# One wait ahead of the loads of the long cross attention

## The chip, the cores and the metric

The kernel runs on one core of a Trainium2 chip. The metric is the device time of one execution in microseconds (us), lower is better. The engines are TensorE (PE, its weight loads shown as PEld), VectorE (DVE), ScalarE (ACT), GpSimd (POOL) and SyncE (SP). SP issues every plain DMA of this kernel, POOL issues the indirect ones (scatters and gathers). All DMAs of both share 16 DMA engines.

## The reference, cut to what matters

Two decoder layers on x (32 batches, 56 tokens, width 128), with a context of 1500 tokens per batch:

```python
x = x + attn0(layernorm(x))                       # stage 0
x = x + cross_attn0(layernorm(x), ctx, ctx, ...)  # stage 1
x = x + experts_top2(layernorm(x), ...)           # stage 2, capacity limited
x = x + running_softmax_attn(layernorm(x), ...)   # stage 3: num/den of cumulative sums
x = x + cross_attn1_rope(layernorm(x), ctx, ...)  # stage 4: the long cross attention, 1500 keys
x = x + experts_sigmoid_top2(layernorm(x), ...)   # stage 5
```

Stage 2 sends each token to two of eight experts and adds up the two results, weighted:

```python
out = ye[idx1, pos1] * (w1 * keep1)[:, None] + ye[idx2, pos2] * (w2 * keep2)[:, None]
```

Stage 3 needs that sum, row by row, before its own layer norm. Stage 4 needs keys and values, which are products of the context alone (`ctx @ Wk.T` with a rotary embedding, `ctx @ Wv.T`).

## The kernel before, in words

The 32 batches are padded to 64 rows and stacked two to a tile, so x is 16 tiles of 128 rows (`XR`). The kernel is written without a planner: each engine has its own program, written out by hand, and `program` walks through the six stages in order on every engine. Where stage k starts, an engine first waits for the end marks of an earlier stage, then runs the *next* stage's preparation (`load` on SP), then stage k's own part. So the loads of stage 4 are issued by SP at the start of stage 3, right behind the last result writes of stage 2 (L1133). The order within SP's queue is the order of the code, and nothing behind a waiting instruction is issued.

**The load of stage 4** (`load` in `l1_xattn`) issues 14 DMAs (L2008), all counted by one semaphore, `c1_in`: five weights of 64 KB, a small mask, the cosine and sine tables (750 KB each), two small tables, and then in pairs `c_ones` (562.5 KB) and `c_zero` (256 KB). Each of these four fills writes 16 partitions alone, with one long row per partition (36,000 and 16,384 bytes). Nine DMAs of the context follow (L2004, `fetch`): three chunks of 250 KB for each of the batches 0, 1 and 2. Every consumer of these loads waits for all 14 (`c1_in(len(loads))`), and the keys and values of batch 0 also for its three context chunks (`ctx_of`).

**The late gathers.** The expert results of stage 2 lie in DRAM (`results`). Two indirect DMAs per tile of rows (L1524, `gather`) fetch them into `XT`, and DVE adds them to `XR` in `combine` (L1383). The tiles 0 to 7 are gathered within stage 2, beside its second half. The tiles 8 to 15 (chunk 1) are gathered in stage 3, by POOL: `LATE_GATHER` says at which step t of stage 3: 0: tiles 8, 9, 10; 1: tiles 11, 12; 2: tiles 13, 14; 3: tile 15. The semaphores `gathered[j]` count tile j and tile j + 8, so `gathered[j](4)` is reached when tile j + 8 has landed as well.

**Stage 3** (`l1_attn`) runs over t = 0 to 19 and keeps one pipeline across the engines: at step t PE projects the values of tile t (L1599), ACT copies them out (L1624), DVE multiplies (L1728) and PE forms running sums (L1672), DVE (L1737, L1741) and POOL (L1795) make the output of tile t - 1, PE turns it (L1683) and multiplies by the output weight (L1691), DVE adds it to `XR` (L1745). DVE also combines the late tiles: 8 and 9 at t = 1, 10 and 11 at t = 2, and so on (`LATE_NORM`). Their norm goes through DVE (L118 to L122), POOL (L127), DVE (L143), PE (L151) and ACT (L156) a step or two later. In POOL's queue an item waits for all items ahead of it: at step t = 2, for instance, the multiply L1795, the four gather DMAs of tiles 13 and 14, and then the norm's power L127 of tiles 8 and 9.

**Early work of stage 4 within stage 3.** From t = 5 on, the engines also run steps of stage 4 (`early`): the keys of batch 0, first chunk, at t = 5 (PE, L2096), values at t = 6 (L2105), the blend with cosine and sine on DVE (L2225) and POOL (L2362, L2368), and so on to t = 19. PE meets the first of them between the transposes of step 5. It is there that PE waits for `c1_in` and for the context of batch 0. SP's own part of stage 3 (`early_sp`) stands behind the loads in its queue. Its first item writes key parts at t = 11 (L2044).

Of the kernel before, what the change touches and what calls it, by code (L numbers as in the profile page):

```python
# [59 lines left out]
def decoder(nc, a, out):  # L60
    with ExitStack() as ctx:
# [5 lines left out]
        def signal(name, total, step=1, over=None):  # L67

            name = over or name
            if name not in sems:  # L70
                sems[name] = [ctx.enter_context(nc.semaphore(name)), 0]
            s = Signal(sems[name][0], sems[name][1], step)
            sems[name][1] += total * step
            return s
# [951 lines left out]
        def l0_ffn():  # L1026
# [65 lines left out]
            gathered = [signal("gathered%d" % j, 4, 16) for j in range(8)]  # L1092
            combine_mul = signal("combine", 2 * NT, over="based")
            combined = lambda t: combine_mul(2 * t + 2)
# [437 lines left out]
            def pool(e, w):  # L1532
                for n in range(16):
                    scatter(e, w, 1, n)
                for j in range(10):
                    if j >= 2:
                        ln_power(e, w, 3, j - 2)
                    if j < 8:
# [1 line left out]

            return Stage(load=load, prep_pool=prep_pool, early_sp=early_sp, early_pe=early_pe, early_dve=early_dve, early_act=early_act,
                         early_pool=early_pool, sp=sp, pe=pe, dve=dve, act=act, pool=pool, gather=gather, combine=combine,
                         combined=combined,
                         end=lambda: [y_cp(NI), down_mm(NI), gated(4 * NI), kept(11), w_cp(NI)] + chunk_out(1))


# [269 lines left out]
        def l1_xattn():  # L1816
# [185 lines left out]
            def fetch(e, b, ch):  # L2002
                sl = slice(500 * ch, 500 * ch + 500)
                e.dma_start(C[:, b % 3, sl], a["ctxT"][b][:, sl]).then_inc(ctx_in[b % 3].sem, 16)  # L2004

            def load(e, w):
                for dst, src in loads:
                    e.dma_start(dst, src).then_inc(c1_in.sem, 16)  # L2008
                for b in range(3):
                    for ch in range(3):  # L2010
                        fetch(e, b, ch)
# [381 lines left out]
            def early_pool(e, w, t, kinds):  # L2393
                for step in early(t):
                    if step[0] in kinds:
                        pool_step(e, w, step)

            return Stage(load=load, chore_pool=chore_pool, between=between, early_sp=early_sp, early_pe=early_pe, early_dve=early_dve,
                         early_act=early_act, early_pool=early_pool, sp=sp, pe=pe, dve=dve, act=act, pool=pool,
                         end=lambda: ln_done(5) + [joined(NT)])  # L2400
# [87 lines left out]
        stages = []  # L2488
        for k, f in enumerate((l0_attn, l0_xattn, l0_ffn, l1_attn, l1_xattn, l1_ffn)):
            place.update(used=642 if k == 5 else 0, low=k % 2 == 0 or k == 5)  # L2490
            stages.append(f())
# [136 lines left out]
```

## Time and profile before

| | us |
|---|---|
| median of 3 runs | 1534.07 |
| lowest, highest | 1530.72, 1545.25 |
| the profiled execution | 1527.03 |
| its span, first to last instruction | 1525.2 |
| mean granted TensorE clock | 0.951 of full |
| PE, DVE, POOL, ACT busy | 89%, 72%, 54%, 54% |

The profiled execution is 7.0 us below the median of the timed runs. Times in the rows are us from the start of the span. `SPq` rows are DMAs that SP issues; their duration is the issue, not the transfer. A number in brackets is the idle time ahead of an instruction, with what ended it. `PEclk` 1.00 is 2.4 GHz and 0.50 is 1.2 GHz. A DMA row gives the median time from issue to landing.

### The profile page before, as it was taken

To read this page: it belongs to the slowest core of one execution; us is meant where nothing else is said; L and a number is where in the kernel's file an instruction comes from. 1 tells how busy PE (TensorE), PEld (TensorE's weight loads), DVE (VectorE), ACT (ScalarE), POOL (GpSimd) and SP (SyncE) were. 2 spreads that over 40 slices of the span, in tenths; PEclk is the share of its full clock that TensorE was granted. 3 is DMA by queue.
4 is the path that set the end of the run, shared out by engine and by line. 5 is a ranking of instruction groups with operands and counts; after the bars stand their busy time and mean duration, and the time that the engine had idled before them with its cause. 6 is when DMAs were issued, how large, how long until landed. Compare 5 with 4: busy or idle time off the path is not lost.

```text
span 1525.2 us, 41823 instructions
## 1 busy us (share of the span) xinstructions
PE 1358.7 (89%) x17179; PEld 927.0 (61%) x17179; DVE 1093.6 (72%) x1832; ACT 821.8 (54%) x1804; POOL 825.7 (54%) x736
## 2 busy tenths in 40 slices
PE   6788999998967996759999999999999999789998
PEld 4567788788935663335666566656665666555554
DVE  6885767656747887747888888888888888435554
ACT  3442334355622331436777777777777777733332
POOL 6665322424654675747778777877787774000000
PEclk9868999999987998779999999999999999989999
DMA  4004400032271034364555554555464554305230
GB/s 128 2 1 128 159 2 2 19 85 86 65 153 39 1 71 78 75 118 124 125 124 133 118 129 123 133 118 132 121 133 118 128 123 93 96 3 111 61 61 13
DMA packets 76511, 134.71 MB, mean 88 GB/s; under 512 B 18017, under 2 KB 56034, under 8 KB 73058
## 3 DMA queue, kind: packets, MB, share of 16 engines
q1 hardware_dynamic: 74274, 127.84, 35.0%
q0 software_dynamic: 2048, 4.20, 1.0%
q8 instruction: 137, 2.24, 0.7%
q14 instruction: 52, 0.43, 0.1%
HBM read 100.54 MB, written 34.73 MB: 89 GB/s over the span
## 4 chain that ended last, share of the span: by engine, by line
PE 35%; POOL 12%; ACT 8%; issue 3%; DVE 3%; DMA 1%; SPq 0%; ACTq 0%; POOLq 0%; DVEq 0%
PE ps L2158 8%; POOL ARENA L2362 8%; PE ps L916 7%; PE ps L2142 5%; POOL ARENA L2368 4%; PE ps L928 4%; PE ps L2105 3%; ACT ARENA L2312 3%; PE ps L2096 2%; ACT ARENA L2290 2%; PE ps L2119 2%; ACT ARENA L2303 2%; ACT ARENA L2296 1%; PE ps L2167 1%; DVE ARENA L2232 1%
## 5 line engine op out<-in xcount | busy, mean ns | idle before, releaser
L2232 DVE TENSOR_REDUCE ARENA<-ps 112x2 f32<-112x1000 f32 x384 | 456.4, 1197 | 122.6 <-PE ps L2119 119.8
L2312 ACT ACTIVATE ARENA<-ps 125x448 f32<-125x448 f32 x768 | 378.4, 549 | 129.0 <-PE ps L2142 128.4
L2362 POOL TENSOR_TENSOR ARENA<-ARENA 64x500 f32<-64x500 f32 x192 | 264.6, 1378 | 106.4 <-ACT ARENA L2290 88.2
L2142 PEld LDWEIGHTS ps<-ARENA 64*125 64x125 bf16 x3072 | 122.9, 134 | 134.6 <-ACT ARENA L2312 70.7
L2142 PE MATMUL ps<-ARENA 64*125 64x112 bf16 x3072 | 169.6, 229 | 19.9 <-ACT ARENA L2312 18.7
L2158 PE MATMUL ps<-ARENA 125*17 125x112 f32 x6144 | 185.5, 261 | 0.0
L2119 PE MATMUL ps<-ARENA 64*112 64x500 bf16 x768 | 153.4, 388 | 9.8 <-DVE ARENA L2232 9.4
L127 POOL TENSOR_TENSOR rs<-rs,mhalf 128x1 f32<-128x1 f32 x96 | 71.7, 750 | 161.1 <-DVE rs L122 160.8
L2158 PEld LDWEIGHTS ps<-ARENA 125*17 125x17 f32 x6144 | 136.7, 97 | 32.1 <-issue 21.9
L2368 POOL TENSOR_TENSOR ARENA<-ARENA 128x500 f32<-128x500 f32 x96 | 147.1, 1533 | 8.1 <-DVE ARENA L2225 0.7
L2373 POOL TENSOR_TENSOR ARENA<-ARENA 128x500 bf16<-128x500 f32 x96 | 111.0, 1157 | 37.7 <-ACT ARENA L2296 37.7
L2096 PE MATMUL ps<-ARENA 128*128 128x500 f32 x192 | 108.2, 647 | 14.6 <-DMA ARENA<-in_ctxT 13.7
L916 PE MATMUL ps<-XT,ARENA 128*128 128x448 f32 x288 | 115.6, 546 | 0.0
L2105 PE MATMUL ps<-ARENA 128*125 128x128 f32 x768 | 109.8, 287 | 1.2 <-ACT ARENA L1624 1.2
L2105 PEld LDWEIGHTS ps<-ARENA 128*125 128x125 f32 x768 | 92.7, 189 | 26.2 <-issue 21.7
L2225 DVE TENSOR_TENSOR ARENA<-ARENA 128x500 f32<-128x500 f32 x96 | 89.8, 935 | 3.5 <-ACT ARENA L2290 3.5
L916 PEld LDWEIGHTS ps<-XT,ARENA 128*128 128x128 f32 x288 | 55.1, 193 | 53.0 <-issue 52.6
L2290 ACT COPY ARENA<-ps 128x500 f32<-128x500 f32 x96 | 55.6, 580 | 48.1 <-PE ps L2096 42.3
L2296 ACT CAST ARENA<-ARENA 128x500 bf16<-128x500 f32 x96 | 58.5, 610 | 35.8 <-POOL ARENA L2368 30.1
L156 ACT COPY XT<-ps 128x128 f32<-128x128 f32 x96 | 25.6, 271 | 91.1 <-PE ps L151 91.1
L1009 DVE TENSOR_TENSOR ARENA<-ps,ARENA 128x448 f32<-128x448 f32 x72 | 44.8, 623 | 41.2 <-PE ps L916 39.8
L789 POOL TENSOR_TENSOR ARENA<-ARENA 128x896 f32<-128x896 f32 x16 | 27.0, 1687 | 81.2 <-DVE ARENA L718 81.2
(273 smaller groups left out, 2384.7 us busy)
## 6 DMA issues: line engine op xcount, KB each, us to landing
ARENA<-key_parts SPq DMA_DIRECT2D x192, 187.5 KB, 3.9
ARENA<-in_ctxT SPq DMA_DIRECT2D x96, 250.0 KB, 3.7
key_parts<-ARENA SPq DMA_DIRECT2D x64, 375.0 KB, 2.6
ARENA<-token_weights SPq DMA_DIRECT2D x16, 512.0 KB, 5.3
slots<-in_c_blank SPq DMA_DIRECT2D x2, 1472.0 KB, 12.5
results<-ARENA SPq DMA_DIRECT2D x42, 64.0 KB, 1.6
ARENA<-in_L_ffn_W SPq DMA_DIRECT2D x1, 2048.0 KB, 8.7
ARENA<-in_L_ffn_W SPq DMA_DIRECT2D x4, 512.0 KB, 10.1
```

The costliest lines, as they stand in the source:

```text
L916: e.matmul(ps[:, bk, 0:448], wt(x, c), rhs, start=True, stop=True).then_inc(up_mm.sem, 1)
L2096: e.matmul(ps[:, b1, 0:500], wk, C[:, b % 3, 500 * ch:500 * ch + 500], start=True, stop=True) \
L2105: m = e.matmul(ps[0:KT, b1, 128 * k:128 * k + 128], C[:, b % 3, KT * kt:KT * kt + KT], wv, start=True, stop=True)
L2119: m = e.matmul(ps[0:112, b1 + h, 0:500], Q0[r, b % 3, g].rearrange("p j s -> p (j s)"), KS[b % 4][r, g, 500 * ch:500 * ch + 500], start=Tr ...
L2142: m = e.matmul(ps[0:KT, b1[h], 112 * g:112 * g + 112], KS[b % 4][r, g, KT * kt:KT * kt + KT], Q1[r, b % 2, 112 * g:112 * g + 112], start=T ...
L2158: m = e.matmul(ps[32 * c:32 * c + 17, 3, 112 * u:112 * u + 112], V[b % 3][0:KT, kt, x, :], Pb[0:KT, n % NP_, 112 * x:112 * x + 112], start ...
L2225: e.tensor_tensor(T1[:, n % 3, :], T0[:, n % 2, :], cos[:, 500 * ch:500 * ch + 500], ALU.mult) \
L2232: e.tensor_reduce(mxp[0:112, b % 2, 2 * g:2 * g + 2, ch], ps[0:112, b1:b1 + 2, 0:500], AX, ALU.max) \
L2312: e.activation(Pb[0:KT, n % NP_, 448 * h:448 * h + 448], ps[0:KT, b1[h], 0:448], ACT.Exp, bias=0.0, scale=1.0).then_inc(exped.sem, 1)
L2362: e.tensor_tensor(T2[r:r + 64, :], T0[64 - r:128 - r, n % 2, :], sin[64 - r:128 - r, sl], ALU.mult) \
L2368: e.tensor_tensor(T1[:, n % 3, :], T1[:, n % 3, :], T2, ALU.add).then_inc(k_sum.sem, 1)
L2373: e.tensor_tensor(Kl[:, sl], T1[:, (3 * b + ch) % 3, :], Kh[:, sl], ALU.subtract).then_inc(k_lo.sem, 1)
```

## The change: eight waits ahead of the loads

Stage 2 publishes a list of eight marks, one for each `gathered` semaphore, at their final count. SP waits for all eight before it issues the first of the 14 loads of stage 4. No load, buffer or size changes, and their order stays.

```diff
@@ l0_ffn
             return Stage(load=load, prep_pool=prep_pool, early_sp=early_sp, ...
-                         combined=combined,
+                         combined=combined, late=lambda: [g(4) for g in gathered],
@@ l1_xattn
             def load(e, w):
+                for mark in stages[2].parts["late"]():
+                    w.wait_ge(*mark)
                 for dst, src in loads:
                     e.dma_start(dst, src).then_inc(c1_in.sem, 16)
                 for b in range(3):
```

## Rows read from the trace of the kernel before

**Rows 1.** The page, busy time of each engine (share of the span), instructions.

```profile
PE 1358.7 (89%) x17179; PEld 927.0 (61%) x17179; DVE 1093.6 (72%) x1832; ACT 821.8 (54%) x1804; POOL 825.7 (54%) x736
```

**Rows 2.** Stretches: start:end, length, busy time of each engine, clock, DMA share, GB/s.

```profile
440.00:455.00 15.00, 5.52 (x9) 1.64 (x7) 5.08 (x10) 1.74 (x3) 11.24 (x11) 0.66 0.89 121
...
470.00:486.00 16.00, 10.10 (x37) 7.37 (x37) 11.23 (x31) 3.24 (x7) 6.82 (x9) 0.68 0.03 8
486.00:503.00 17.00, 16.64 (x95) 11.67 (x95) 13.73 (x26) 6.59 (x14) 8.34 (x8) 1.00 0.00 1
```

**Rows 3.** Chain that ended last: start, duration, engine and line.

```profile
582.73 1.80 PE ps L1691 x16
```

**Rows 4.** Timeline of SP's issues: start, duration, line.

```profile
427.58 0.33 SPq L2008 DMA_DIRECT2D ARENA<-in_L_xattn_WqT  x1
...
434.08 0.44 SPq L2008 DMA_DIRECT2D ARENA<-in_c_zero  x1
434.57 11.98 SPq L2004 DMA_DIRECT2D ARENA<-in_ctxT  x9
```

**Rows 5.** DMA issues about 434.2, 435.6, 432.2 and 470.2: us to landing last.

```profile
ARENA<-in_c_zero SPq DMA_DIRECT2D x1, 256.0 KB, 20.7
...
ARENA<-in_ctxT SPq DMA_DIRECT2D x1, 250.0 KB, 22.1
...
XT<-results,IDX POOLq DMA_INDIRECT x1, 14.2
...
XT<-results,IDX POOLq DMA_INDIRECT x1, 2.5
```

**Rows 6.** Timeline of DVE, the late combine and what stands around it.

```profile
437.68 1.22 DVE L1741 TENSOR_TENSOR ARENA<-ARENA 128x1024 f32<-128x1024 f32 x1 [0.73 <-POOL ARENA L1795]
...
446.39 0.74 DVE L1383 SCALAR_TENSOR_TENSOR XR<-XT,GW,XR 128x128 f32<-128x128 f32 x2 [6.10 <-DMA XT<-results,IDX]
...
458.95 1.36 DVE L143 TENSOR_SCALAR xn<-XR,mv,rs 128x128 f32<-128x128 f32 x2 [7.56 <-POOL rs L127]
```

**Rows 7.** Timeline of POOL, from the gather of tile 10 to that of tile 15.

```profile
437.73 2.03 POOL L1524 DMA_INDIRECT XT<-results,IDX  x1
...
451.53 1.90 POOL L1795 TENSOR_TENSOR ARENA<-ARENA 128x1024 f32<-128x1024 f32 x1 [2.17 <-DVE ARENA L1741]
...
458.32 1.10 POOL L127 TENSOR_TENSOR rs<-rs,mhalf 128x1 f32<-128x1 f32 x2
...
466.73 1.90 POOL L1795 TENSOR_TENSOR ARENA<-ARENA 128x1024 f32<-128x1024 f32 x1 [6.58 <-DVE ARENA L1741]
...
470.10 0.96 POOL L1524 DMA_INDIRECT XT<-results,IDX  x1 [0.30 <-issue]
```

**Rows 8.** Timeline of PE about its restart and about the first keys.

```profile
460.38 0.45 PE L151 MATMUL ps<-ident,xn 128*128 128x128 f32 x1 [6.36 <-DVE xn L143]
...
461.45 1.91 PE L1683 MATMUL ps<-ident,ARENA 128*128 128x128 f32 x8
463.16 2.78 PE L1691 MATMUL ps<-ARENA 128*128 128x128 f32 x16
...
486.11 1.01 PE L2096 MATMUL ps<-ARENA 128*128 128x500 f32 x2
...
487.07 1.03 PE L1683 MATMUL ps<-ident,ARENA 128*128 128x128 f32 x8
487.95 2.05 PE L1691 MATMUL ps<-ARENA 128*128 128x128 f32 x16
```

**Rows 9.** Finer stretches, the columns of rows 2.

```profile
457.50:460.00 2.50, 0.00 (x0) 0.00 (x0) 1.05 (x2) 0.00 (x0) 2.49 (x4) 0.61 1.05 367
460.00:462.50 2.50, 1.76 (x7) 1.50 (x8) 2.29 (x10) 0.53 (x2) 0.15 (x1) 0.50 0.50 181
462.50:465.00 2.50, 2.50 (x15) 2.50 (x14) 2.43 (x5) 1.17 (x2) 0.00 (x0) 0.52 0.00 0
465.00:467.50 2.50, 2.50 (x14) 1.54 (x13) 2.36 (x6) 0.00 (x0) 0.77 (x1) 1.00 0.00 0
```

## The prediction

> **What bounds the kernel now.** I read the page first. PE is busy 89% of the span [rows 1], but an average over six stages doesn't price a change at the border of two, so I went to the stretch that it touches: stretches of time from the end of stage 2 on, then each engine's timeline there, then the landings of the DMAs. Three things are to be seen. Between 440 and 486 us PE is far from full (5.5 of 15 us, then 10.1 of 16), while from 486 to 503 it is busy 16.6 of 17 us [rows 2]. The boundary is the first key product, at 486.11 us [rows 8]: ahead of it PE waits for others, behind it PE sets the pace. Second, the chain that ended last, followed back, is still in stage 3's own products (L1691) at 582.7 [rows 3], and stage 3's steps are a pipeline two buffers deep, so a delay of PE at 486 goes through to the end. Third, SP issues the stage 4 loads from 427.58 on [rows 4], far ahead of their first use.
>
> **What these loads cost now.** The second gather of tile 9 is issued at about 432.2 and takes 14.2 us to land, against 2.5 us for the last one of tile 15, issued when nothing else moves [rows 5]. DVE pays: its combine of tile 9 starts at 446.39 after 6.10 us of waiting for that landing [rows 6]. That is the only wait for a late gather that I find; the others land before DVE comes to them.
>
> **What the change gives back.** Without the loads beside it, that gather lands near 435, and DVE goes on 6.1 us sooner. But only part of it reaches the rest: the next thing in line is POOL's multiply L1795 at 451.53, which waited only 2.17 us for DVE and is behind POOL's own gathers otherwise [rows 7]. From there the chain is one of POOL's queue: gathers of tiles 13 and 14, then the power of tile 8's norm (458.32), then DVE's L143 at 458.95 (idle 7.56 us for POOL), then DVE's add, the multiply at 466.73, and the gathers of tile 15 [rows 6, 7]. So all of it moves by 2.17 us, not 6.1. A second gain is possible: the gather issue at 437.73 took 2.03 us where the last takes 0.96 [rows 7], which would make it 3.2 us if the busy DMA rings were the reason. It ran, however, exactly beside DVE's L1741, which starts at 437.68 and lasts 1.22 us [rows 6], and that stays. So I take 2.0 us as the gain at the moment at which tile 15 is gathered: the 2.17, and a little off. The bounds are 3.2 and 0, the latter if two such collisions of 1.1 us come in where DVE used to wait beside the gathers of tiles 11 and 12. The Trainium skill ("SBUF — State Buffer", SBUF: two separate sides) says that GpSimd and a DVE instruction with two SBUF inputs take turns on a shared port, the second one blocked until the first ends. By that rule the 1.1 us stay, and the sum would be nearer to the bound of 0; if it doesn't hold here, 3.2.
>
> **What the change costs.** The eight waits end with the last: `gathered[7]`, tile 15. Its second DMA is issued at 470.10 and lands 2.5 us on, at 472.6 [rows 5, 7]. With the gain it is 470.6. SP has nothing else queued there until the key parts of t = 11, so the waits cost nothing themselves; the semaphore hop I cost at 0.1, so the first load is issued at 470.7 instead of 427.58.
>
> How long from the first issue to usable data? Before, `c_zero`, the last of the 14, is issued at 434.08 and lands 20.7 us on, at 454.8. The third context chunk is issued two places behind 434.57, near 435.5, and lands 22.1 us on, at 457.6 [rows 4, 5]. Measured from the first issue that is 27.2 us for `c1_in` and 30.0 us for the context of batch 0, which PE needs too. Now the late gathers are out of the way. Ten DMAs of 64 KB (tiles 8 to 12) had landed by 457.6, 0.66 MB. At 367 GB/s, the rate at which contexts stream at 457.5 to 460 [rows 9], they are 1.8 us; at the mean 121 GB/s of 440 to 455 [rows 2] they would be 5.4 us. The low mean comes, I read, from the four fills, whose 16 long rows give each DMA engine one row of each fill, one behind the other, and these stay. So 28.2 us, with 24.6 and 30.0 as bounds.
>
> The key product then starts at 470.7 + 28.2 = 498.9 instead of 486.11: 12.8 us late. PE, which comes to it about 2 us earlier than before, stands idle from about 484 to 499. That is a new stall of some 15 us where 6.1 us of another engine's waiting was removed. DVE, POOL and ACT run out of work within a step, since step 6 needs step 5's products.
>
> **The clock after the stall** comes on top. When PE restarts at 460.38 after 6.4 us idle, the granted clock is 0.50 and then 0.52, and 1.00 from 465 on [rows 8, 9]. In that time eight transposes take 1.91 us and sixteen products 2.78, against 1.03 and 2.05 at full clock [rows 8]: 1.6 us for the two groups. As all the 4.6 us from restart to full clock would be dense now, at most 2.3 us are lost. I take 2.0.
>
> **The sum.** 12.8 + 2.0 = 14.8 us. The profiled execution of 1527.0 becomes 1541.8. It is 7.0 us under the median of the runs shown, 1534.1, so the median comes to 1548.9. Bounds of the case: 472.7 - 3.2 + 24.6 = 494.1 gives 8.0, with 1.6 for the clock 9.6 us; 472.7 + 30.0 = 502.7 gives 16.6, with 2.3 it is 18.9 us. So 1543.7 to 1553.0 as median.
>
> **The rivals.**
>
> *The loads land in time, and the kernel is not slower.* PE reaches the key product at 484.1, and SP starts at 470.7: the loads need 13.4 us or less. The loads and the first context are 4.37 MB, which at the 367 GB/s of [rows 9] is 11.9 us, and no stall is left; the gain of 2.0 us stands: 1525.0 in the profile, 1532.1 as median. The Trainium skill ("DMA: Bandwidth & Descriptors", Anatomy of one DMA) gives a fixed 2.0 us plus bytes at 436 GB/s, which makes 12.0 us and speaks for this rival. Against it stands the same list of DMAs in this trace: 30.0 us, when the gathers beside it moved only 0.66 MB. The rule would have to hold for 36,000-byte rows into 16 partitions. It decides at 13.4 us. Chance 0.07.
>
> *The stall is longer and the clock stays down.* The gathers of tile 15 come no sooner than before (collisions take all), the loads take the full 30.0 us, and PE, which alternates between short bursts and waits after the restart, is granted 0.50 for a whole step instead of 4.6 us. A stretch for it exists: between 470 and 486 PE was busy 10.1 of 16 us, and the clock averaged 0.68 [rows 2]. Price: 472.7 + 30.0 - 486.1 = 16.6 us, and a step of 8 us at half clock 4 us, 20.6 us: 1547.6 in the profile, 1554.7 as median. Against it: behind the stall PE is fed densely, as at 486 to 503. Chance 0.2.
>
> *Part is made up later.* Once PE restarts, DVE, POOL and ACT have caught up, and stage 3's last steps, where PE isn't full, swallow some of it. For it speaks that the gain of 6.1 us of DVE's is lost in just that manner. Against: a step ahead is all that two buffers allow. Price: half of the 12.8 us gone, +8.4 us, 1535.4 in the profile and 1542.5 as median. Chance 0.13.
>
> That the change does nothing is hardly possible: tile 15 is gathered after 468 in any case, SP would have to pass a semaphore that isn't there yet.
>
> **How the numbers follow.** The forecast of 1549 us has 0.6. One per cent is 15.3 us, about what a measurement of this kernel tells from no change, and 14.8 lies right under it; with the bounds of the terms and the spread of the runs (1530.7 to 1545.3) I give 0.45 of this case to over 1%. Slower by over 1%: 0.6 x 0.45 + 0.2 = 0.47. Within 1%: 0.33 + 0.13 + most of the first rival, 0.05: 0.51. Faster: 0.02. The range goes from 1539, under the case of partial recovery (1542.5) by what low runs may take off, to 1559, above the long stall.
>
> **What would show it.** In the trace of the changed kernel: SP's first L2008 near 470.7 instead of 427.58; the gather of tile 9 landing within 3 us and no idle time before L1383; POOL's multiply near 449.5 instead of 451.53, and the gather of tile 15 near 468; the idle time before PE's first L2096 near 15 us, put down to the context or the tables, with L2096 near 499; a clock of 0.50 for about 4.6 us behind it; and from there every instruction 14 to 15 us later than before, to the end. If the loads take a time far from 28 us, the term of the fills is wrong, and the result with it. If L2096 starts near 499 and the end moves by less than 12, the coupling of stage 3 is looser than I hold it to be.

## The result: 0.8% slower, 12 us at the median

| | before | changed |
|---|---|---|
| median of 20 runs, us | 1533.76 | 1545.97 |
| lowest, highest, us | 1523.82, 1545.25 | 1542.69, 1555.13 |
| profiled execution, us | 1527.03 | 1545.08 |
| its span, us | 1525.2 | 1543.3 |

The ratio is 1.0081, with a 95% interval of 1.0059 to 1.0104: 9 to 16 us slower. The forecast was 1548.9 us at the median, 14.8 us over the kernel before. The two profiled executions differ by 18.1 us, more than the medians do. How much of that is the change is taken apart below. One execution of the kernel before in a later group of runs took 1734.58 us at a mean granted clock of 0.734, where the others have about 0.95; it is in no median and no ratio here.

The profile after, from its page: the busy time of PE is 1360.4 us where [rows 1] had 1358.7, so the change adds no work, only waiting.

```profile
PE 1360.4 (88%) x17179; PEld 924.7 (60%) x17179; DVE 1096.3 (71%) x1832; ACT 821.7 (53%) x1804; POOL 825.0 (53%) x736
```

The stretches of the changed kernel that answer to [rows 2], and one more:

```profile
440.00:455.00 15.00, 6.25 (x16) 2.36 (x13) 7.63 (x12) 2.09 (x3) 13.16 (x12) 0.70 0.11 31
...
470.00:486.00 16.00, 9.52 (x37) 6.80 (x37) 12.26 (x34) 3.52 (x8) 6.20 (x9) 0.79 0.82 178
486.00:503.00 17.00, 3.76 (x12) 2.69 (x13) 3.18 (x3) 1.33 (x3) 2.92 (x3) 0.53 0.88 185
503.00:518.00 15.00, 14.64 (x83) 10.70 (x83) 8.86 (x19) 4.77 (x9) 5.59 (x5) 0.97 0.00 1
```

Between 486 and 503 us PE was busy 16.64 of 17 us; now it is 3.76, while the DMAs move 185 GB/s. SP's queue and the landings show why. The timeline of SP in the changed kernel, and the landings of the DMAs issued near 478.7 (`c_zero`) and 480.1 (third context chunk):

```profile
471.97 0.33 SPq L2010 DMA_DIRECT2D ARENA<-in_L_xattn_WqT  x1
...
479.08 8.06 SPq L2004 DMA_DIRECT2D ARENA<-in_ctxT  x9
```

```profile
ARENA<-in_c_zero SPq DMA_DIRECT2D x1, 256.0 KB, 18.6
...
ARENA<-in_ctxT SPq DMA_DIRECT2D x1, 250.0 KB, 19.1
```

The first load is issued at 471.97, not 427.58 [rows 4]. The third context chunk lands near 499.2, and PE's timeline has its first key product right there:

```profile
499.24 2.01 PE L2098 MATMUL ps<-ARENA 128*128 128x500 f32 x2 [14.17 <-issue]
501.04 0.42 PE L151 MATMUL ps<-ident,xn 128*128 128x128 f32 x1
501.25 1.92 PE L1683 MATMUL ps<-ident,ARENA 128*128 128x128 f32 x8
502.96 2.47 PE L1691 MATMUL ps<-ARENA 128*128 128x128 f32 x16
505.26 1.88 PE L1599 MATMUL ps<-ARENA,XT 128*128 128x512 f32 x4
```

Against [rows 8] the product starts at 499.24 instead of 486.11, after 14.17 us of idle time. The profile puts these down to "issue", not to a DMA; that the context lands at the same moment is what tells. The product, the transposes (L1683) and the output products (L1691) take 2.01, 1.92 and 2.47 us, where they took 1.01, 1.03 and 2.05 at full clock.

What the wait gives back is seen on DVE and POOL. First the timeline of DVE, with the combine of tiles 8 and 9 (L1383) without idle time, then that of POOL:

```profile
440.93 0.73 DVE L1383 SCALAR_TENSOR_TENSOR XR<-XT,GW,XR 128x128 f32<-128x128 f32 x2
...
442.31 3.17 DVE L1728 TENSOR_TENSOR ARENA<-ARENA 128x1024 f32<-128x1024 f32 x1
...
458.29 1.36 DVE L143 TENSOR_SCALAR xn<-XR,mv,rs 128x128 f32<-128x128 f32 x2 [10.39 <-POOL rs L127]
```

```profile
429.07 0.99 POOL L1524 DMA_INDIRECT XT<-results,IDX  x1 [5.61 <-DMA results<-ARENA]
...
442.48 1.91 POOL L1795 TENSOR_TENSOR ARENA<-ARENA 128x1024 f32<-128x1024 f32 x1
444.55 1.80 POOL L1524 DMA_INDIRECT XT<-results,IDX  x1 [0.16 <-issue]
...
450.83 1.92 POOL L1795 TENSOR_TENSOR ARENA<-ARENA 128x1024 f32<-128x1024 f32 x1
...
469.46 0.96 POOL L1524 DMA_INDIRECT XT<-results,IDX  x1 [0.30 <-issue]
```

The first late gather is at 429.07, where it was at 428.36: the changed kernel comes 0.71 us later to this border, by nothing that the change touches. With that taken off, POOL's multiply at 450.83 is 1.41 us earlier than in [rows 7], and so is the rest up to the last gather of tile 15 (469.46 for 470.10, 1.35 us). In [rows 6] DVE waited 6.10 us for the gather and 7.56 us for POOL ahead of L143, 13.66 us together; now it is 10.39 us for POOL alone. At PE's key product the gain is a little larger than at the gathers: PE is ready for it at about 484.9 instead of 486.1, which is 1.9 us earlier with the border taken off.

### The profile page after: what moved, and what is told of

Its sections match the earlier page's. It is cut to its first block, busy times and chain, and to the rows that moved or that the text cites. A ratio compares the mean times of both kernels' runs of the same rounds, so it can differ in the third digit from the quotient of the medians.

```text
span 1543.3 us, 41827 instructions
## 1 busy us (share of the span) xinstructions
PE 1360.4 (88%) x17179; PEld 924.7 (60%) x17179; DVE 1096.3 (71%) x1832; ACT 821.7 (53%) x1804; POOL 825.0 (53%) x736
## 4 chain that ended last, share of the span: by engine, by line
PE 36%; POOL 11%; ACT 8%; issue 3%; DVE 2%; DMA 1%; SPq 0%; ACTq 0%; POOLq 0%; DVEq 0%
PE ps L2160 8%; POOL ARENA L2364 7%; PE ps L916 7%; PE ps L2144 5%; POOL ARENA L2370 4%; PE ps L928 4%; ACT ARENA L2314 3%; PE ps L2107 3%; PE ps L2098 2%; ACT ARENA L2292 2%; PE ps L2121 2%; ACT ARENA L2305 1%; ACT ARENA L2298 1%; PE ps L2169 1%; DVE ARENA L2234 1%
## 5 line engine op out<-in xcount | busy, mean ns | idle before, releaser
L2370 POOL TENSOR_TENSOR ARENA<-ARENA 128x500 f32<-128x500 f32 x96 | 147.3, 1534 | 8.1 <-DVE ARENA L2227 0.7
L2098 PE MATMUL ps<-ARENA 128*128 128x500 f32 x192 | 110.7, 661 | 27.2 <-issue 14.2
L151 PE MATMUL ps<-ident,xn 128*128 128x128 f32 x80 | 27.3, 349 | 55.6 <-DVE xn L143 48.4
```

The lines of the kernel that those rows point to most:

```text
L2098: e.matmul(ps[:, b1, 0:500], wk, C[:, b % 3, 500 * ch:500 * ch + 500], start=True, stop=True) \
L2370: e.tensor_tensor(T1[:, n % 3, :], T1[:, n % 3, :], T2, ALU.add).then_inc(k_sum.sem, 1)
```

## The experiments

All are compared with the kernel before, run beside them on the same chip. As times of whole executions scatter, each profile is also read over one stretch that holds the change and ends when the clock is full again: from the first late gather (POOL, first L1524 of chunk 1) to the first values of batch 0 (PE, `values` at t = 6). Before, that is 428.36 to 494.07, 65.71 us.

| kernel | first late gather | first values | stretch, us | against before | ratio of times, 95% interval |
|---|---|---|---|---|---|
| before | 428.36 | 494.07 | 65.71 | | |
| changed | 429.07 | 509.49 | 80.42 | +14.7 | 1.0081 (1.0059 to 1.0104) |
| changed, again | 431.79 | 511.98 | 80.19 | +14.5 | 1.0123 (1.0077 to 1.0168) |
| wait for tiles 8 to 14 | 437.98 | 507.37 | 69.39 | +3.7 | 1.0016 (0.9992 to 1.0039) |
| wait for tiles 8 to 12 | 438.97 | 503.02 | 64.05 | -1.7 | 1.0005 (0.9980 to 1.0029) |
| wait for tiles 8, 9 | 428.56 | 494.26 | 65.70 | 0.0 | 1.0035 (1.0008 to 1.0061) |
| all waits, fills last | 437.26 | 501.61 | 64.35 | -1.4 | 1.0006 (0.9978 to 1.0033) |
| no wait, fills last | 428.44 | 494.58 | 66.14 | +0.4 | 1.0017 (0.9995 to 1.0040) |
| changed, 30 products in the stall | 440.30 | 530.00 | 89.70 | +24.0 | 1.0142 (1.0113 to 1.0172) |
| changed, 15 products in the stall | 428.42 | 510.86 | 82.44 | +16.7 | 1.0084 (1.0055 to 1.0114) |
| changed, 18 products in the stall | 429.39 | 509.61 | 80.22 | +14.5 | 1.0089 (1.0057 to 1.0121) |

**Is it the length of the wait?** Fewer tiles are waited for, one line of the change:

```diff
-                         combined=combined, late=lambda: [g(4) for g in gathered],
+                         combined=combined, late=lambda: [g(4) for g in gathered[:5]],
```

> SP waits for the five tiles 8 to 12 alone (gathered[0] to gathered[4]) instead of all eight. Theory (the cost is a start that is too late for a load that takes 27.2 us): tile 12 has landed near 451.6 in the changed kernel, so the loads start near 451.7 and the context of batch 0 is there near 479, before PE comes to its first key product near 485. No stall there, the gain of 0.7 to 1.5 us of the gathers stays, the time is that of the kernel before or up to 2 us under it: ratio 0.998 to 1.001. Rival (the waits in SP's queue or the loads beside stage 3's compute cost in themselves, wherever they stand): still a ratio of 1.004 or more, with PE's first key product near 485 all the same.

Measured: ratio 1.0005, interval 0.998 to 1.0029. SP issues the first load at 461.60, which is 22.6 us behind the first late gather instead of 42.9, and PE goes into the key product with no gap:

```profile
494.40 0.33 PE L151 MATMUL ps<-ident,xn 128*128 128x128 f32 x1 [0.36 <-ACT XT L156]
494.57 1.01 PE L2098 MATMUL ps<-ARENA 128*128 128x500 f32 x2
```

Waits in SP's queue cost nothing as such, and the loads beside stage 3's compute cost nothing that the times can tell. The interval ends below the rival's 1.004, so the rival is out. The stretch is 1.7 us shorter, as expected; that is 0.1% of the time, under what the ratio can show. The next one waits for all but tile 15 (`gathered[:7]`).

> SP waits for tiles 8 to 14 (gathered[0] to gathered[6]), all but tile 15. Theory: tile 14 has landed near 459.2, plus 27.2 us makes 486.4 for the context of batch 0, against PE's arrival near 485: a stall of 1 to 2 us, that cancels the gain; ratio 0.999 to 1.002. Gathers of tile 15 issue at 468 beside the fills and land up to 14 us late, near 484, where DVE wants them near 484: at most 2 us more. Rival (a wait of any length costs as much as all eight): ratio near 1.008.

Measured: ratio 1.0016. SP's first load is at 468.22, the key product starts 28.8 us later, and both costs that were named are there, a stall of PE of 3.40 us and one of DVE for tile 15's gather of 2.27 us. The timelines of PE and DVE:

```profile
497.04 2.00 PE L2098 MATMUL ps<-ARENA 128*128 128x500 f32 x2 [3.40 <-issue]
```

```profile
495.20 0.74 DVE L1383 SCALAR_TENSOR_TENSOR XR<-XT,GW,XR 128x128 f32<-128x128 f32 x2 [2.27 <-DMA XT<-results,IDX]
```

The stretch is 3.7 us longer, where I expected up to 2 and up to 2 more: the load took 28.8 us instead of 27.3. The loads start 30.2 us behind the first late gather instead of 42.9, and these 12.7 us remove 11.0 of the 14.7: where the load is on the path, its start counts in full, and the 1.5 us between the two are the longer load.

**What makes up the 27 us of loading?** All eight waits stay, and the four fills move behind the contexts, with a semaphore of their own:

```diff
-            loads += [x for r in (48, 112) for x in (ones(KSa, r), (QS[r:r + 16]..., a["c_zero"]))]
+            fills = [x for r in (48, 112) for x in (ones(KSa, r), (QS[r:r + 16]..., a["c_zero"]))]
+            fill_in = signal("fill_in", len(fills), 16)
@@ load, behind the nine fetches
+                for dst, src in fills:
+                    e.dma_start(dst, src).then_inc(fill_in.sem, 16)
@@ pe of stage 4, and its mask on POOL
+                w.wait_ge(*fill_in(len(fills)))
```

> All eight waits stay. The four fills of 16 partitions (the ones and the zeros) are issued behind the nine context DMAs and have a semaphore of their own, which only stage 4 waits for (PE's own part and POOL's masks). Theory (the 27.2 us are mainly the four fills, each engine moving their long rows one behind the other): the other ten loads and the first context, 2.7 MB, are there 10 to 13 us after the first issue at 472, near 482 to 485, PE's first key product starts near 485 to 487, and 12 us of the 14 come back: ratio 0.998 to 1.001. Rival (issue by SP, or the bytes, or DRAM set the load time): 2.7 of 4.4 MB take 17 us or more, the product starts near 489 or later, and a ratio of 1.003 or more is left.

Measured: ratio 1.0006. SP's timeline, and PE's:

```profile
480.17 0.33 SPq L2011 DMA_DIRECT2D ARENA<-in_L_xattn_WqT  x1
485.15 4.62 SPq L2005 DMA_DIRECT2D ARENA<-in_ctxT  x9
489.81 0.45 SPq L2016 DMA_DIRECT2D ARENA<-in_c_ones  x1
```

```profile
493.10 0.33 PE L151 MATMUL ps<-ident,xn 128*128 128x128 f32 x1 [0.35 <-ACT XT L156]
493.26 1.01 PE L2101 MATMUL ps<-ARENA 128*128 128x500 f32 x2
```

The landing of the third context chunk, issued near 486.1:

```profile
ARENA<-in_ctxT SPq DMA_DIRECT2D x1, 250.0 KB, 4.9
```

The first load is issued at 480.17, and 13.1 us later PE passes the same wait with no idle time. The data were there before PE was: the third context chunk landed near 491.0, 10.8 us behind the first load. In the changed kernel the same tables and context landed after 27.2 us. So 16 of the 27 us are the fills ahead of the contexts, and the stall is theirs: with them out of the way, all eight waits cost nothing that the times can tell, and the stretch is 1.4 us shorter than before.

It isn't the bytes alone. Tables and first context, 2.70 MB in 10.8 us, make 250 GB/s; at that rate the 1.68 MB of the fills would take 6.7 us, not 16. What in their shape costs so much, no run separates: they have long rows, and they write 16 partitions. The trace speaks against the length alone: the packets of 36,000 bytes take 5.0 us at the median in the kernel before, those of 47,104 bytes, with which the buffer `slots` in DRAM is blanked, 1.8 us.

**Is the gain DVE's 6.1 us?** Only tiles 8 and 9 are waited for (`gathered[:2]`).

> SP waits for tiles 8 and 9 alone, whose gathers are the only ones that DVE waited for. Theory: they land near 435, the loads start there and are complete near 463, 20 us ahead of their use; DVE's 6.1 us of idle time is gone, the rest of the late gathers run beside the loads again and land 10 to 16 us after issue, still ahead of their use. Stage 3 comes to its first key product 0.7 to 1.5 us earlier than in the kernel before, which is under what the times can tell: ratio 0.998 to 1.001. Rival (the removed DVE wait is worth its 6.1 us): ratio 0.996.

Measured: ratio 1.0035, interval 1.0008 to 1.0061, a little over what I gave it; the stretch is the same as before to 0.01 us. The expected 0.7 to 1.5 us aren't there. DVE's timeline shows where they went: the combine of tile 9 no longer waits, but that of tile 11 does, for a gather issued while the fills run. The DMA issues near 446.4 (tile 11) give its time to landing:

```profile
440.41 0.73 DVE L1383 SCALAR_TENSOR_TENSOR XR<-XT,GW,XR 128x128 f32<-128x128 f32 x2
459.03 0.72 DVE L1383 SCALAR_TENSOR_TENSOR XR<-XT,GW,XR 128x128 f32<-128x128 f32 x2
461.74 0.74 DVE L1383 SCALAR_TENSOR_TENSOR XR<-XT,GW,XR 128x128 f32<-128x128 f32 x2 [1.26 <-DMA XT<-results,IDX]
```

```profile
XT<-results,IDX POOLq DMA_INDIRECT x1, 15.6
```

The wait for one gather was traded for a wait for another. My expectation that they land ahead of their use was wrong by 1.3 us. Since this profile is as long as that of before (span 1525.7 for 1525.2), the 0.35% of the times aren't in it, and I can't say what they are.

**Fills last, without any wait**, is the same edit on the kernel before.

> The kernel before, without any of the eight waits, with the four fills of 16 partitions issued behind the context DMAs under their own semaphore. Theory (tile 9's gather was late because it stood behind the fills' long rows and the tables): with tables and contexts alone ahead of it, it lands 4 to 9 us after its issue and not 14, DVE's idle time of 6.1 us ahead of the combine of tile 9 shrinks to 0 to 1 us; the gathers of tiles 10 to 12 now meet the fills and land 10 to 15 us after issue, near their use. Stage 3 comes to its key product 0 to 1.5 us earlier than before, ratio 0.998 to 1.001. Rival (the bytes ahead of it, not the long rows, delay the gather): it lands at 446 as before and nothing moves.

Measured: ratio 1.0017, no difference that can be told. Tile 9's gather no longer holds DVE up: its combine runs at 440.30, 6.1 us earlier than before, and its gather lands 5.7 us after issue instead of 14.2, with tables and contexts ahead of it. So the fills, and not any bytes ahead of it, had delayed it. But tile 11's does, as with the wait for two tiles:

```profile
462.38 0.74 DVE L1383 SCALAR_TENSOR_TENSOR XR<-XT,GW,XR 128x128 f32<-128x128 f32 x2 [1.97 <-DMA XT<-results,IDX]
```

**What does the clock cost after the stall?** The changed kernel, with products without use ahead of the wait:

```diff
                 elif kind == "keys":
                     ch = step[2]
+                    if (b, ch) == (0, 0):
+                        w.wait_ge(*free[b1])
+                        for _ in range(30):
+                            e.matmul(ps[:, b1, :], ident[:, :], XT[1][:, 0:512], start=True, stop=True)
+                        w.wait_ge(*c1_in(len(loads)))
                     w.wait_ge(*ctx_of(b))
@@ early_pe
-                    w.wait_ge(*c1_in(len(loads)))
+                    if step != ("keys", 0, 0):
+                        w.wait_ge(*c1_in(len(loads)))
```

> The changed kernel with 30 extra matrix products of 512 columns, with no use, on PE ahead of its first early key product, into the bank that this product overwrites; at 0.43 us each they fill 13 of the 14 us for which PE waits there. Theory: the data arrive as before, the product starts near 499.2 again, but the granted clock is 1.00 and not 0.50 when it does, so the 2.5 us that the restart at half clock costs come back: 2 to 3 us less than the changed kernel, a ratio of 1.006 against the kernel before where the changed one has 1.008. Rival (the stall alone is the cost, the clock costs nothing): the same 1.008; or, if the extra work delays the product, more.

A miss: ratio 1.0142, interval 1.0113 to 1.0172, and the stretch 24.0 us longer than before. I had taken the 0.43 us of one record for one product; a product of 512 columns in this type is two records. The 30 of them ran for 25.91 us and held up the key product themselves. With 15 in place of 30:

> The changed kernel with 15 extra matrix products of 512 columns, with no use, on PE ahead of its first early key product, into the bank that this product overwrites. In the run with 30 of them each took 0.86 us and the 25.9 us overran the wait; 15 take 13.0 us of its 14. Theory: the context lands as before, the key product starts within 1 us of where it does in the changed kernel, counted from the first load, but at a granted clock of 1.00; its two matrix products take 1.0 instead of 2.0 us and the step behind it is 2.5 us shorter: 2 to 3 us less than the changed kernel, ratio 1.006 against 1.008 for that one. Rival (the clock costs nothing that reaches the end): the same ratio as the changed kernel.

Measured: ratio 1.0084, and still half clock at the restart. The context landed 28.5 us after the first load, later than in the changed kernel, and left PE idle for 3.05 us behind the filler. The timeline of PE and the clock of that stretch:

```profile
483.89 13.04 PE L2099 MATMUL ps<-XT,ident 128*128 128x512 f32 x30
499.99 2.00 PE L2103 MATMUL ps<-ARENA 128*128 128x500 f32 x2 [3.05 <-DMA ARENA<-in_ctxT]
```

```profile
497.00:499.50 2.50, 0.00 (x0) 0.00 (x0) 0.00 (x0) 0.00 (x0) 0.00 (x0) 0.95 1.04 386
499.50:502.00 2.50, 2.02 (x4) 0.94 (x4) 0.00 (x0) 0.00 (x0) 0.00 (x0) 0.50 0.94 349
```

The third has 18:

> As the kernel with 15 idle-filling products, with 18 of them: 15.7 us, so that PE goes from the last of them into the key product with no gap, where 15 left 3.05 us of idle time and the product began at half clock all the same. Theory: the clock is 1.00 at the key product and behind it (two products in 1.0 us, sixteen L1691 in 2.05), and what stage 3 is late by against the changed kernel falls by up to 2.5 us, less what the filler overruns the landing by (0 to 1.5 us). The times can hardly tell: ratio 1.006 to 1.010. Rival (half clock is caused by something else than the idle time): 2.0 us and 2.5 us again for the two groups.

Measured: ratio 1.0089. Now 0.80 us are left idle and the clock stays at 1.00. PE's timeline and the clock of its restart:

```profile
485.17 15.62 PE L2099 MATMUL ps<-XT,ident 128*128 128x512 f32 x36
501.58 1.08 PE L2103 MATMUL ps<-ARENA 128*128 128x500 f32 x2 [0.80 <-DMA ARENA<-in_ctxT]
502.50 0.27 PE L151 MATMUL ps<-ident,xn 128*128 128x128 f32 x1
502.61 1.03 PE L1683 MATMUL ps<-ident,ARENA 128*128 128x128 f32 x8
503.49 2.05 PE L1691 MATMUL ps<-ARENA 128*128 128x128 f32 x16
```

```profile
499.50:502.00 2.50, 1.70 (x5) 0.52 (x4) 0.00 (x0) 0.00 (x0) 0.00 (x0) 1.00 1.05 386
```

From the key product to the first values it is 8.03 us (501.58 to 509.61), the 7.96 of before (486.11 to 494.07), against 10.25 in the changed kernel (499.24 to 509.49). So the half clock costs 2.3 us, shown. It didn't shorten the stretch, because this time the context landed 29.1 us after the first load. Whether the filler made the DMAs slower isn't settled, but it looks so: with all eight waits and no late gather beside the loads, the third context chunk landed 27.2 and 26.7 us after the first load without the filler, and 28.1, 28.5 and 29.1 us with 30, 15 and 18 products. The runs with fewer waits, where late gathers move beside the loads, had 27.7 and 28.7 us without a filler.

**How well does a profile repeat?** The two kernels once more, unchanged.

> The changed kernel on the chip of the other kernels of this call. Theory: ratio 1.006 to 1.010. The wait of PE ahead of its first early key product is 14 us again and the loads take 27 to 28 us from the first issue to that product, since both are set by the order of the queues. Rival (the 27 us were an accident of one run): they differ by over 2 us.

Measured: ratio 1.0123 from six runs. The stall is 13.66 us, and the product starts 26.8 us behind the first load (474.69 to 501.46): within a microsecond of the first profile.

> The kernel before once more, with a profile of its own, as the measure of what two runs of one program differ by. Theory: ratio 1.000 within its interval; step 5's key product starts 58.5 us behind the first load, as before; the end of the profile against that product moves by up to 4 us with the clock that is granted between stages 3 and 4. Rival (the first profile of before was typical in all its parts): its span is the first profile's 1525 us but for one constant shift at the start.

Measured: ratio 1.0007, interval 0.9984 to 1.0030. The only profile taken of it has a span of 1732.8 us, so nothing in it can be compared, and what I expected of the key product and of the stretch between stages 3 and 4 is untested by it. The kernel before has one usable profile; that the kernel with waits for tiles 8 and 9 has the same stretch to 0.01 us is what speaks for it.

## Why the prediction was right

**The mechanism and its place hold.** SP's start hangs on tile 15, the first load goes out 0.1 us after the last gather has landed, and PE pays at its first key product. The runs with fewer tiles show how the cost grows: none up to tile 12, 3.7 us up to tile 14, 14.7 with all.

**The gain, taken as 2.0 us at the gathers of tile 15, was 1.4.** The part that POOL's queue lets through was read rightly: 6.1 us of DVE, of which 2.17 at most could count. The collisions that I kept for the bound came: with DVE no longer idle, POOL's gather of tile 11 took 1.80 us, where it took 0.99 before by the same profile, and DVE's L1728 took 3.17 for 1.21, with POOL's multiply beside it until 444.39. The 2.17 us less the 0.8 of that gather are the 1.4. The 2.03 us of the gather issue at 437.73, which had a second gain to give, stayed 2.03 in the changed kernel (at 438.45) with no load in flight. The Trainium skill ("SBUF — State Buffer", SBUF: two separate sides) says that the second of two such instructions on the shared port waits for the first to end. In all three the times add up so, for instance 1.91 and 1.21 us to 3.17. The order agrees for the two gathers; but L1728's record begins 0.17 us before that of POOL's multiply, and yet it was DVE that waited.

**The load, taken as 28.2 us, was 27.3** (471.97 to 499.24). The four other profiles in which PE waited for these loads have 26.8 to 29.3 up to the product. The reading that the fills dominate is now shown by the run that moves them. The rate rule of the first rival, which would have had all data there in 12 us, fails here for these loads. The Trainium skill ("DMA: Bandwidth & Descriptors", Anatomy of one DMA) gives it for one DMA issued by GpSimd; the prediction laid it over 17 DMAs of SP. For the tables and the first context alone the same sum is 8.2 us, an estimate by that page, and the run with the fills last took 10.8.

**The clock, taken as 2.0 us, was 2.3**, by the difference between 10.25 and 7.96 us, and the run with 18 products gives it back. It is the prediction's upper estimate, the whole time at half clock spent on dense work.

**The sum of the stretch:** 13.1 us at the product (499.24 - 486.11), less 0.71 of the later border, and 2.3 of the clock are 14.7; forecast 14.8. The stretch repeats at 14.5. That the two agree to 0.1 us is partly luck: with the border taken off, the first load went out 0.6 us later than forecast, the load took 0.9 less and the clock cost 0.3 more. At the median the change costs 12.2 us, 2.6 less than forecast, and the interval of 9 to 16 holds 14.7. It doesn't settle whether 2 us are made up somewhere.

**The 18.1 us of the two profiles** are another matter. At 582.73 of [rows 3] the changed kernel is at 597.80, 15.1 us late. The next stretches, before and changed, show the clock falling at a different moment at the border of stages 3 and 4:

```profile
585.00:600.00 15.00, 9.28 (x30) 4.75 (x30) 10.94 (x24) 1.14 (x3) 4.12 (x7) 0.89 0.42 121
```

```profile
600.00:615.00 15.00, 10.38 (x26) 5.75 (x26) 8.32 (x19) 0.87 (x2) 2.37 (x4) 0.60 0.42 121
```

The stretch with the same work was granted 0.89 and then 0.60. The lateness grows from 15.1 us to 18.1 at the next key products (598.55 and 616.66) and 19.4 at those behind them (601.38 and 620.77). At a wait for the context it is down to 16.7 (687.50 and 704.24, after 13.68 us idle before and 11.80 in the changed kernel), and it ends at 18.1. So the sign "every instruction 14 to 15 us later to the end" did not hold in this profile.

One group shows the border best: the L1691 products behind the second query products of stage 4 (L2089 before, L2091 in the changed kernel). They took 2.44 us before and 3.79 in the changed kernel. Of the six profiles in which PE stalled or ran products without use, four have 3.78 or 3.79 and two less (2.05 with 15 products, 2.48 with 30). Of the five without a stall, one has 3.78, the one with waits for tiles 8 to 12, and four have 2.05 to 2.44. So the slow border can come without the stall and be absent with one. I count these 3 us to the scatter of the clock, but they were commoner where PE had stalled, and no run excludes that the stall makes them likelier.

**The rivals.** That loads land in time failed at the fills. That part is made up later isn't seen in stage 3, where the lateness is 15.4 us at the first values and 15.1 at the end. The longer stall with a clock that stays down didn't come: PE was fed densely and had full clock from 505 on.

## What to carry to other kernels

A load that is held back until other traffic has passed costs its start plus its own time against its first use; take that time from the trace of the same list of DMAs, since bytes over the rate gave 12 us here and the queue took 27. Look at the shape of what stands at the head of the queue: four fills of 16 partitions took 16 us of it, and with them behind the urgent loads the whole wait cost nothing that the times could tell. And when a wait of one engine is removed, ask whose turn is next: of 6.1 us of DVE waiting, POOL's queue let 1.4 through to the last gathers, and with shorter waits the next late gather took the rest.

## What the runs showed of the hardware

- Four writes of 16 partitions with one long row each (36,000 and 16,384 bytes) take 16 us of the DMA queue for 1.7 MB (27.2 us to the context with them ahead, 10.8 with them behind), and beside them an indirect DMA of 64 KB on another queue takes 10 to 16 us to land instead of 2.5.
- PE idle for 3.05 us started again at a granted clock of 0.50, idle for 0.80 us at 1.00.
- The same code ahead of the change takes different time: the first late gather comes at 428.4 to 431.8 us in seven of the profiles, and at 437.3 to 440.3 in the four that were run together on one chip, on which the kernel before has a median of 1542.65 instead of 1530 to 1534 us. In one of these four, ACT and DVE wait 8.2 and 10.4 us in stage 2 for something that the profile calls remote. What it is stays open. Differences under 1% between profiles of different chips are therefore read over a stretch, and not over the span.
